# Building two one-hot groups within the head, and gate logits on VectorE, in a graph layer with a mixture of experts

## The chip, the cores and the metric

The kernel runs on one core of one Trainium2 chip. The metric is the device time of one execution in microseconds (us). A core has TensorE (PE in the profile), VectorE (DVE), ScalarE (ACT), GpSimd (POOL) and SyncE (SP, which only issues DMAs here). Each engine takes its instructions in order; they wait for one another through semaphores.

## What is computed

```python
def layernorm(x): return (x - mean(x)) / sqrt(var(x) + 1e-5)      # over the 256 features
# x [3125, 256]; src, dst [50000], sorted by dst; edge_weight [50000]
msgs = layernorm(x)[src] * edge_weight[:, None]
agg = segment_sum(msgs, dst, 3125)
x = x + agg @ W.T + b                                            # W [256, 256]
z = layernorm(x)
gates = softmax(z @ gW + gb)                                     # 4 experts
topv, topi = top_k(gates, 2); topw = softmax(topv)
shared = mlp(z; 256 -> 256 -> 128 -> 256, relu)
experts = mlp_e(z; 256 -> 128 -> 64 -> 256, relu), e = 0..3
x = x + shared + sum over the two chosen experts of topw * expert
```

All of it is float32.

## The kernel before, in words

**Tiles and units.** The 3,125 nodes are 25 tiles of 128. They are worked in 14 units of one or two tiles: G0 to G9 (the first 2,229 nodes, "gathered") and D0 to D3 ("dense"). The order of the units is `UNIT_ORDER`, "G0 D0 G1 G2 D1 G3 G4 G5 D2 G6 G7 G8 D3 G9".

**Head.** SP loads x in groups; PE multiplies x by the centred weight (L1098), ScalarE scales the product by each row's 1/std (L906) into `xn_all` and stores it as a table in DRAM (L866). VectorE takes the row statistics (`statistics(g)`, L1402, L1406), counts where each window of edges begins (`count_smaller`, with PE's `count`), and checks the edges (`edge_faults`). `choose_path` writes a flag for which all engines wait.

**Gathered units.** GpSimd gathers the source rows of 12 chunks of 128 edges (one batch; the last batch has 6): three batches of raw x (L818), then 21 from the table (L834), 246 gathers. The rows have a ring of three batches: batch b waits for `s_used`, which PE raises in batch b - 3. VectorE makes for each batch a selector (`selectors`, L1581, L1585) and a placement (L1593); PE multiplies both (`select_batch` L1155, `merge` L1191). The raw batches also need row statistics (`row_statistics`, L1532, L1536, for 12 chunks) and two transposing steps (`rawturn`, `rawlin`).

**Dense units.** For each window of five nodes SP loads a record of 128 edges (L741, 1.5 KB in 128 short pieces). VectorE splits a block of records into keys (`split_records`, L1601 to L1622). For each group of four windows VectorE makes `high_node` (`onehots`, L1635) and ScalarE `low_1h` (`low_halves`, L920, L924), PE multiplies them (`build_group`, L1209), ScalarE copies the result into `dense` (`copy_built`, L970), and PE multiplies `dense` by `xn_all` (`multiply`, L1222). Dense unit 0 has 13 groups and is multiplied tile by tile: its first 25 products need groups 0 to 6. Record blocks are of 16 windows (`BLOCKS`).

**After the sum** every unit goes through residual, statistics, `norm` (L1678), `turn` (L1234), `xt` (L989), `gated` (gate logits, L1244, on PE), layers 1 to 3 (L1264, L1273, L1277, L1311 to L1314), and on VectorE `route` (L1689 to L1694), `rank`, `mix`, `turned`, `weigh`, `finish`.

**The order of the work.** What each engine does after the flag is a list that `schedule()` (L181) works out when the kernel is built: it takes the steps' costs, start times and due times (`done`, `free`) and ranks (`RANKS`), and picks step by step. The engines run their list in order, without looking ahead. What stands ahead of the lists is written by hand: on VectorE `split_records(0)`, onehots 0 and 1, row statistics, shifts, selectors and placement of batch 0 (after `choose_path`); on ScalarE `low_halves` 0 and 1 and `row_deviation(0)` after the last table store. PE builds groups 0 and 1 as the first items of its list.

```python
            load_records(0)
            sp.dma_start(src_all[:, 0:N_CHUNKS - 1], src).then_inc(s_src, 16)
            sp.dma_start(w_all[:, 0:N_CHUNKS - 1], wgt).then_inc(s_wgt, 16)
            load_records(1)
            sp.wait_ge(s_table, 16 * len(groups))
```

Of the kernel before, what the change touches and what calls it, by code (L numbers as in the profile page):

```python
# [6 lines left out]
P = 128  # L7
# [69 lines left out]
         for v in range(4)]  # L77
WINDOWS = [-(-u.tok // WIN) for u in DENSE]
# [55 lines left out]
def users_of(b):  # L134
# [4 lines left out]
BLOCKS = [(v, t0, min(BLOCK, LOADED[v] - t0)) for v in range(len(DENSE))  # L139
          for t0 in range(0, LOADED[v], BLOCK)]  # L140
# [18 lines left out]
def block_of(v, g):  # L159
    return [(w, t0 // BLOCK) for w, t0, _ in BLOCKS].index((v, g * GROUP // BLOCK))  # L160


BANKS = 2
EARLY, FORE = 2, 4
# [5 lines left out]
RANKS = {"open": 3, "near": 0.105, "behind": 0.46, "dve_behind": 0.83, "act_behind": 1.65, "hurry": -2.49,  # L170
         "batch": 5.25, "rawturn": 14.77, "rawlin": -17.2, "merge": 7.43, "windows": 19.55, "built": 0.44,
         "rowstd": 15.95, "rawxt": -2.24, "rawout": 12.98, "low": 22.59, "select": 3.55,
         "select_late": -1.3, "place": -20.25, "records": 11.53, "onehot": -3.9, "rowstats": 5.81,
         "rowshifts": -8.25}
BUILD_RANKS = (2.58, 16.22, -1.26, -10.69)
MULT_RANKS = (-5.54, -8.91, 10.79, 17.88)
# [4 lines left out]
def schedule():  # L181
# [7 lines left out]
    done, units, left = {("load", 0): 31.0, ("load", 1): 46.0, ("load", 2): 59.5, ("load", 3): 62.5, ("records", 0): 36.0,  # L189
            ("select", 0): 46.0, ("place", 0): 46.2}, [], {}  # L190
    done.update({("begin", v): 28.5 for v in range(1, len(DENSE))})
    done.update({("onehot", k): 37.4 + 1.1 * k for k in range(EARLY)})
    done.update({("low", k): 39.3 + 1.9 * k for k in range(EARLY)})
# [3 lines left out]
    nxt = {"batch": 0, "windows": 0, "select": 1, "place": 1, "build": 0, "built": 0, "onehot": EARLY, "low": EARLY,  # L197
           "records": 1, "mult": 0, "load": FORE, "store": 0, "rowstats": 1, "rowstd": 1, "rowshifts": 1,
# [30 lines left out]
    def unit_steps(u):  # L229
        q, T, half = units.index(u), u.T, max(0.42, u.tok / PAIR)  # L230
        one = units[q - 1] if q else None
# [15 lines left out]
        else:  # L247
# [7 lines left out]
            ("dve", "norm", 0.33 * T, lambda: needs(of("std"), prior("turn", one))),  # L255
# [166 lines left out]
def build(nc, x, x_cols, src, src_tail, dst, dst_tail, nxt, nxt_tail, wgt, wgt_tail, rec, gnn_wt, packed, every, out, force_general=False):  # L422
# [5 lines left out]
    with ExitStack() as ctx:  # L428
# [249 lines left out]
        def built_in(k):  # L678

            if k % BANKS == 0:  # L680
                return build_ps
# [13 lines left out]
        def stores_before(n):  # L695
            return sum(stores_of(unit) for unit in UNITS[:n])
# [1239 lines left out]
```

## Time and profile before

| | us |
|---|---|
| median of 3 runs (lowest, highest) | 399.25 (397.38, 399.33) |
| profiled execution, whole | 398.72 |
| its span, first to last instruction | 396.6 |

```profile
PE   4998579999999999999999999999999999899984
PEld 3786457868787888888796877787878877767772
DVE  6659998984799698514688455462175442446541
ACT  2554795494388788504999532322049231244331
POOL 7777777777777777777777777777777777772000
PEclk9998668999999999999999999999999999999999
DMA  6999745944444544543343434343433344332000
```

The span is cut into 40 slices of 9.9 us; a digit is the busy share of a slice in tenths (9 is 90% or more), PEclk the granted TensorE clock in tenths of full speed. PEld is PE's loading of weights, which runs beside PE.

### The profile page before, as it was taken

The numbers are of one execution on the slowest core, as the hardware profiler recorded it, in microseconds if no ns is written. First come the engines' busy times: TensorE is split into PE (matmuls) and PEld (weight loads), VectorE is DVE, ScalarE is ACT, GpSimd is POOL, SyncE is SP. The second block draws the span as 40 slices with busy tenths as digits, with TensorE's granted clock in tenths as the row PEclk, the third lists the DMA queues.
The fourth block names the chain that finished last, engine by engine and source line by source line (L and its number), as shares of the span: only waits on it lengthen the run. The fifth ranks groups of instructions, "written<-read, shape, count | busy, mean of one in ns | idle before, by whom it ended". The sixth has DMA issues, their size and how long they took to land.

```text
span 396.6 us, 8051 instructions
## 1 busy us (share of the span) xinstructions
PE 367.7 (93%) x2419; PEld 295.9 (75%) x2419; DVE 243.5 (61%) x1013; ACT 202.0 (51%) x551; POOL 273.5 (69%) x294
## 2 busy tenths in 40 slices
PE   4998579999999999999999999999999999899984
PEld 3786457868787888888796877787878877767772
DVE  6659998984799698514688455462175442446541
ACT  2554795494388788504999532322049231244331
POOL 7777777777777777777777777777777777772000
PEclk9998668999999999999999999999999999999999
DMA  6999745944444544543343434343433344332000
GB/s 183 379 380 279 210 111 131 341 106 105 105 108 118 129 118 100 133 106 108 104 130 102 132 107 134 105 129 105 132 103 107 115 125 134 105 108 80 15 13 25
DMA packets 53855, 53.15 MB, mean 134 GB/s; under 512 B 32522, under 2 KB 43636, under 8 KB 53684
## 3 DMA queue, kind: packets, MB, share of 16 engines
q0 software_dynamic: 13536, 36.98, 31.8%
q1 hardware_dynamic: 35220, 10.01, 10.9%
q10 hardware_dynamic: 5056, 5.64, 4.1%
q8 instruction: 21, 0.34, 0.4%
q14 instruction: 22, 0.18, 0.1%
HBM read 46.12 MB, written 6.48 MB: 133 GB/s over the span
## 4 chain that ended last, share of the span: by engine, by line
PE 82%; ACT 6%; DMA 5%; DVE 3%; issue 2%; SPq 1%; ACTq 0%; DVEq 0%
PE agg_ps L1222 19%; PE hid_ps L1264 17%; PE window_ps L1155 8%; PE tok_ps L1313 5%; DMA x_sb<-in_x 5%; PE build_ps L1209 5%; PE agg_ps L1191 5%; PE agg_ps L1209 4%; PE tok_ps L1311 3%; PE hid_ps L1277 3%; PE hid_ps L1273 3%; PE mid_ps L1244 3%; ACT low_1h L920 2%; PE hid_ps L1209 2%; PE mid_ps L1234 1%
## 5 line engine op out<-in xcount | busy, mean ns | idle before, releaser
L834 POOL DMA_INDIRECT rows<-normalised_rows,src_all x246 | 236.2, 960 | 75.5 <-issue 74.3
L1222 PE MATMUL agg_ps<-xn_all,dense 128*128 128x256 f32 x350 | 80.3, 381 | 0.8 <-ACT dense L970 0.8
L1222 PEld LDWEIGHTS agg_ps<-xn_all,dense 128*128 128x128 f32 x350 | 65.3, 190 | 11.0 <-ACT dense L970 1.7
L1264 PE MATMUL hid_ps<-xt,pack 128*128 128x256 f32 (+2 forms) x336 | 71.4, 358 | 0.0
L1264 PEld LDWEIGHTS hid_ps<-xt,pack 128*128 128x128 f32 x336 | 56.4, 190 | 9.1 <-issue 3.6
L920 ACT ACTIVATE low_1h<-iota,lo_f 128x128 f32<-128x128 f32 x182 | 57.6, 393 | 0.5 <-ACT xn_all L906 0.5
L1635 DVE TENSOR_SCALAR high_node<-iota,hi_f,own_w 128x125 f32<-128x125 f32 x182 | 49.4, 357 | 4.5 <-PE build_ps L1209 2.9
L1008 ACT ACTIVATE h<-hid_ps,pack 128x256 f32<-128x256 f32 (+2 forms) x84 | 32.8, 441 | 37.4 <-PE hid_ps L1264 37.2
L818 POOL DMA_INDIRECT rows<-in_x,src_first x36 | 34.9, 968 | 11.0 <-issue 10.4
L1155 PE MATMUL window_ps<-rows,select 128*32 128x256 f32 x564 | 37.3, 394 | 0.9 <-DVE select L1585 0.9
L1209 PE MATMUL build_ps<-high_node,low_1h 128*128 128x125 f32 x184 | 27.8, 299 | 4.6 <-ACT low_1h L924 3.6
L1209 PEld LDWEIGHTS build_ps<-high_node,low_1h 128*128 128x128 f32 x184 | 25.5, 212 | 7.9 <-issue 5.6
L924 ACT ACTIVATE low_1h<-low_1h 128x512 f32<-128x512 f32 (+1 forms) x46 | 28.8, 626 | 1.5
L1155 PEld LDWEIGHTS window_ps<-rows,select 128*32 128x32 f32 x564 | 16.5, 112 | 15.3 <-issue 5.2
L1799 DVE TENSOR_TENSOR y<-tok_ps,x 128x512 f32<-128x512 f32 (+1 forms) x14 | 8.9, 633 | 28.6 <-PE tok_ps L1314 28.6
L1313 PE MATMUL tok_ps<-pack,h 128*128 128x256 f32 (+1 forms) x100 | 25.7, 378 | 0.0
L970 ACT ACTIVATE dense<-build_ps 128x500 f32<-128x500 f32 x23 | 14.6, 636 | 20.7 <-PE agg_ps L1222 18.6
L1581 DVE TENSOR_TENSOR select<-slots,rel 128x384 f32<-128x384 f32 (+1 forms) x24 | 13.2, 550 | 15.8 <-PE window_ps L1155 15.7
L951 ACT ACTIVATE windows<-window_ps 128x256 f32<-128x256 f32 (+1 forms) x24 | 9.1, 378 | 25.8 <-PE window_ps L1155 25.8
L1191 PE MATMUL agg_ps<-windows,place 128*128 128x256 f32 (+1 forms) x92 | 21.8, 382 | 0.0
L1313 PEld LDWEIGHTS tok_ps<-pack,h 128*128 128x128 f32 (+1 forms) x100 | 18.7, 187 | 3.0
L1191 PEld LDWEIGHTS agg_ps<-windows,place 128*128 128x128 f32 (+1 forms) x92 | 16.9, 190 | 2.3 <-issue 0.3
(172 smaller groups left out, 523.2 us busy)
## 6 DMA issues: line engine op xcount, KB each, us to landing
rows<-normalised_rows,src_all POOLq DMA_INDIRECT x246, 2.8
x_sb<-in_x SPq DMA_DIRECT2D x6, 512.0 KB, 9.0
normalised_rows<-xn_all ACTq DMA_DIRECT2D x6, 512.0 KB
records<-in_rec SPq DMA_DIRECT2D x184, 1.5 KB
out<-y SPq DMA_DIRECT2D x10, 256.0 KB
dense<-in_x_cols ACTq DMA_DIRECT2D x4, 512.0 KB, 9.9
pack<-in_packed SPq DMA_DIRECT2D x1, 1544.5 KB, 9.9
x_sb<-in_x SPq DMA_DIRECT2D x3, 256.0 KB
```

What stands on the lines that cost most here:

```text
L818: pool.indirect_dma_start(rows[:, b * BATCH + pos, :], None, x[:, :], bass.IndirectOffsetOnAxis(ap=src_first[:, c:c + 1], axis=0)).then_in ...
L834: pool.indirect_dma_start(rows[:, b % RING * BATCH + pos, :], None, table[:, :], bass.IndirectOffsetOnAxis(ap=src_all[:, c:c + 1], axis=0) ...
L920: last = act.activation(low_1h[:, k % RING, j, :], iota[:, 0:P], ACT.Abs, scale=-1.0, bias=lo_f[:, at + j:at + j + 1])
L924: act.activation(low_1h[:, k % RING, 0:n, :], low_1h[:, k % RING, 0:n, :], ACT.Relu, scale=-1.0, bias=1.0).then_inc(s_low, 1)
L1008: last = act.activation(u.h1[:, m, 0:tok], by_half(u.hid_ps[k % 2])[:, m % 2, 0:tok], ACT.Relu, bias=b1_sb[:, m:m + 1])
L1155: last = pe.matmul(window_ps[SLOT * g:SLOT * (g + 1), 0:D], select[:, b % RING, j, :], rows[:, b % RING * BATCH + pos, :], start=(i == 0), ...
L1191: last = pe.matmul(sums_of(unit)[:, t * D:(t + 1) * D], place[0:full, b % KEEP, at:at + P], windows[0:full, b % KEEP, :], start=(b == batc ...
L1209: last = pe.matmul(built_in(k)[:, j * width:(j + 1) * width], low_1h[:, k % RING, j, :], high_node[:, k % RING, j, :], start=True, stop=True)
L1222: last = pe.matmul(dense_ps[0:r, t * D:(t + 1) * D], dense[:, h, t * P:t * P + r], xn_all[:, h, :], start=(h == 0 and t == 0), stop=(h == ...
L1264: last = pe.matmul(by_half(u.hid_ps[b % 2])[:, m % 2, 0:tok], w, u.xt[:, k, 0:tok], start=(k == 0), stop=(k == KD - 1))
L1313: pe.matmul(o, u.h2[:, 1 + k, c], ew3_sb[:, k, :], start=False, stop=False)
L1635: last = dve.tensor_scalar(high_node[:, r, j, :], iota[:, 0:HI * WIN], hi_f[:, at + j:at + j + 1], own_w[:, at + j:at + j + 1], ALU.is_equ ...
```

## The change

It does four things:

1. Record blocks: the first block of 16 windows becomes two of 8 (`HEAD_BLOCK`), so there are 15 blocks. SP issues the same loads in the same order (blocks 0 and 1 ahead of src and w, block 2 behind them, block 3 after the table).
2. On VectorE `split_records(0)` and `onehots(0)` now stand between `statistics(5)` and `statistics(6)`, `onehots(1)` behind `statistics(6)`; after `choose_path` come `split_records(1)`, `row_statistics(0)`, `onehots(2)`, `row_shifts(0)`, `selectors(0)`, `placement(0)`. On ScalarE `low_halves(0)` stands ahead of the last deviation, `low_halves(1)` ahead of the scaling of product 11; after the flag come two `copy_built`, `low_halves(2)` and `row_deviation(0)`. PE builds group 0 behind the product of pair 10 and ahead of `count(3)`, group 1 behind the last product. Three groups are one-hot ahead of the lists instead of two.
3. The gate logits of all units but D3, G8 and G9 (`LAST_UNITS`) are made on VectorE, four `tensor_tensor_reduce` of 256 elements a tile, with the bias as start value; `gated` on PE and the bias add in `route` go away for these eleven units (21 tiles). The transposed gate weights come with the broadcast load `shared`, which grows from 130 KB to 642 KB.
4. The lists are made anew, with other ranks and start times. They begin so (unit or number behind each step):

```
PE before:  build 0, 1, batch 0, build 2, 3, rawturn 0, rawlin 0, build 4, 5, 6, batch 1, mult 0 (25 of them),
            build 7, 8, 9, batch 2, build 10, batch 3, rawturn 1, build 11, rawlin 1, build 12, merge G0, batch 4, mult 0 (25)
PE after:   build 2, batch 0, build 3, rawturn 0, rawlin 0, build 4, 5, batch 1, build 6, 7, rawturn 1, mult 0 (2), rawlin 1,
            mult 0 (23), batch 2, build 8, batch 3, build 9, 10, 11, batch 4, merge G0, build 12, rawturn 2, ...
DVE before: onehot 2, 3, records 1, rowstats 1, onehot 4, 5, rowshifts 1, onehot 6, 7, select 1, place 1, rowstats 2, ...
DVE after:  onehot 3, rowstats 1, records 2, rowshifts 1, onehot 4, 5, 6, select 1, place 1, onehot 7, rowstats 2,
            records 3, rowshifts 2, onehot 8, bias G0, onehot 9, 10, select 2, place 2, ...
ACT after:  low 3, built 2, windows 0, built 3, rawxt 0, rowstd 1, rawout 0, low 4, 5, 6, built 4, 5, low 7, windows 1,
            rowstd 2, built 6, 7, rawxt 1, ...
```

In the list after, the steps of G0 stand among the second 25 products of unit 0 (before: behind them), and all steps of G2 up to `spr` ahead of the products of unit 1 (before: up to `l1b`). From batch 22 on both lists of PE are the same.

```diff
+LAST_UNITS = [DENSE[-1], *GATHERED[-2:]]
+HEAD_BLOCK = 2 * GROUP
+BLOCKS = [(0, t0, HEAD_BLOCK) for t0 in range(0, BLOCK, HEAD_BLOCK)]
+BLOCKS += [(v, t0, min(BLOCK, LOADED[v] - t0)) for v in range(len(DENSE))
+           for t0 in range(0 if v else BLOCK, LOADED[v], BLOCK)]
-EARLY, FORE = 2, 4
+EARLY, FORE = 3, 5
-    free = {"pe": 36.6, "act": 44.9, "dve": 46.2, "sp": 65.0}
+    free = {"pe": 39.2, "act": 44.1, "dve": 46.1, "sp": 65.0}
...
+    done.update({("onehot", k): (30.0, 32.5, 44.8)[k] for k in range(EARLY)})
+    done.update({("low", k): (31.4, 37.6, 42.5)[k] for k in range(EARLY)})
...
-            ("pe", "gated", 0.24 * T, lambda: needs(of("xt"))),
+        ] + ([
+            ("pe", "gated", 0.41 * T, lambda: needs(of("xt"))),
+        ] if late else []) + [
...
+            ("dve", "gates", 1.63 * T, lambda: needs(of("norm"))),
...
-        row_stats = sb("row_stats", [P, ROW_SLOTS, 6])
+        row_stats = dst_i[:, 0:6 * ROW_SLOTS].bitcast(F32).rearrange("p (j s) -> p j s", s=6)
...
+            if GROUPS[k][0] < TILE_BY_TILE:
+                return u.hid_ps[k % BANKS]
+            return dense_ps if k % BANKS else build_ps
...
-                sp.dma_start(shared[:, :], every.to_broadcast([P, D + E])).then_inc(s_linear, 16)
+                sp.dma_start(shared[:, :], every.to_broadcast([P, D + E * D + E])).then_inc(s_linear, 16)
...
             load_records(0)
+            load_records(1)
             sp.dma_start(src_all[:, 0:N_CHUNKS - 1], src).then_inc(s_src, 16)
             sp.dma_start(w_all[:, 0:N_CHUNKS - 1], wgt).then_inc(s_wgt, 16)
-            load_records(1)
+            load_records(2)
             sp.wait_ge(s_table, 16 * len(groups))
...
+                if p == 9:
+                    low_halves(0)
                 if p in DEVIATIONS:
                     deviations(DEVIATIONS.index(p))
+                if p == len(pairs) - 1:
+                    low_halves(1)
...
-            for k in range(EARLY):
-                low_halves(k)
-            row_deviation(0)
+            act.wait_ge(s_flag, 1)
+            for k in range(BANKS):
+                copy_built(k)
+            low_halves(BANKS)
+            row_deviation(0)
...
                 multiply_x(p)
+                if p == 10:
+                    build_group(0)
                 if p == 1:
                     count(0)
...
+            build_group(1)
             pe.wait_ge(s_flag, 1)
...
+            def gates(q):
+                done = E * gated_tiles(q)
+                dve.wait_ge(s["xn"], q + 1)
+                for t in range(UNITS[q].T):
+                    for e in range(E):
+                        if done >= 2:
+                            dve.wait_ge(s_gate_x, done - 1)
+                        dve.tensor_tensor_reduce(
+                            out=gate_x[:, done % 2, :], in0=u.xn[:, t, :], in1=gate_w_sb[:, e, :], scale=1.0,
+                            scalar=gate_b_sb[:, e:e + 1], op0=ALU.mult, op1=ALU.add,
+                            accum_out=u.logit[:, t, e:e + 1]).then_inc(s_gate_x, 1)
+                        done += 1
...
             statistics(5)
             split_records(0)
-            for k in range(EARLY):
-                onehots(k)
+            onehots(0)
+            statistics(6)
+            onehots(1)
+            edge_places()
+            count_smaller(3)
+            edge_faults()
+            for v in range(1, len(DENSE)):
+                begin_windows(v)
+            choose_path()
+            split_records(1)
             row_statistics(0)
+            onehots(2)
             row_shifts(0)
             selectors(0)
             placement(0)
```

## Rows read from the trace of the kernel before

**Rows 1.** the page, parts 1 and 5: busy time; the gathers (busy, mean ns).

```profile
PE 367.7 (93%) x2419; PEld 295.9 (75%) x2419; DVE 243.5 (61%) x1013; ACT 202.0 (51%) x551; POOL 273.5 (69%) x294
...
L834 POOL DMA_INDIRECT rows<-normalised_rows,src_all x246 | 236.2, 960 | 75.5 <-issue 74.3
```

**Rows 2.** timeline of PE (start us, us): one unit's gate products; batch 23.

```profile
315.07 0.95 PE L1244 MATMUL mid_ps<-pack,xt 128*128 128x4 f32 x8
315.88 1.97 PE L1264 MATMUL hid_ps<-xt,pack 128*128 128x256 f32 x8
...
369.48 1.49 PE L1155 MATMUL window_ps<-rows,select 128*32 128x256 f32 x12
```

**Rows 3.** the same 246 gathers by line: ns min/median/max; landing.

```profile
L834 POOL DMA_INDIRECT rows<-normalised_rows,src_all x246: 941/946/1287, 49.4 to 359.7; - x123
...
DMA to landing us min/median/max: 2.7/2.8/3.8
```

**Rows 4.** timeline of POOL: three of its gathers.

```profile
49.36 0.95 POOL L834 DMA_INDIRECT rows<-normalised_rows,src_all  x1 [0.36 <-PE window_ps L1155]
...
82.95 1.23 POOL L834 DMA_INDIRECT rows<-normalised_rows,src_all  x1 [0.30 <-issue]
...
359.75 0.95 POOL L834 DMA_INDIRECT rows<-normalised_rows,src_all  x1 [0.30 <-issue]
```

**Rows 5.** timeline of DVE in the head, with what ended its idle time.

```profile
29.54 1.41 DVE L1402 BATCH_NORM_STATS2 stats<-x_sb 128x6 f32<-128x256 f32 x4 [3.00 <-DMA x_sb<-in_x]
...
31.28 0.42 DVE L1480 SCALAR_TENSOR_TENSOR rel<-dst_f,tok_ps 128x282 f32<-128x282 f32 x1
...
37.71 0.15 DVE L1601 TENSOR_SCALAR hi_i<-records 128x16 int32<-128x16 int32 x1
...
38.89 2.14 DVE L1635 TENSOR_SCALAR high_node<-iota,hi_f,own_w 128x125 f32<-128x125 f32 x8
40.95 4.00 DVE L1532 BATCH_NORM_STATS2 row_stats<-rows 128x6 f32<-128x256 f32 x12
...
46.51 0.17 DVE L1544 TENSOR_TENSOR row_w<-w_all,row_rstd 128x12 f32<-128x12 f32 x1 [0.62 <-ACT row_rstd L875]
...
47.84 0.34 DVE L1593 TENSOR_SCALAR place<-iota,posn 128x256 f32<-128x256 f32 x1
```

**Rows 6.** SP's record loads; DMA queue 1 in 27:31 and in 31:36 us.

```profile
17.05 9.24 SPq L741 DMA_DIRECT2D records<-in_rec  x8
...
q1 hardware_dynamic: 907, 0.04, 14.5%
...
q1 hardware_dynamic: 1150, 0.01, 13.5%
```

**Rows 7.** timeline of ACT in the head.

```profile
39.72 1.02 ACT L906 ACTIVATE xn_all<-build_ps,zero,rstd 128x256 f32<-128x256 f32 x2 [1.64 <-PE build_ps L1098]
...
41.21 1.28 ACT L920 ACTIVATE low_1h<-iota,lo_f 128x128 f32<-128x128 f32 x4 [0.47 <-ACT xn_all L906]
42.52 0.63 ACT L924 ACTIVATE low_1h<-low_1h 128x512 f32<-128x512 f32 x1
```

**Rows 8.** timeline of PE, head and first product of dense unit 0.

```profile
43.25 2.04 PE L1209 MATMUL build_ps<-high_node,low_1h 128*128 128x125 f32 x8 [3.56 <-ACT low_1h L924]
...
47.98 2.79 PE L1155 MATMUL window_ps<-rows,select 128*32 128x256 f32 x24 [0.86 <-DVE select L1585]
...
65.42 11.06 PE L1222 MATMUL agg_ps<-xn_all,dense 128*128 128x256 f32 x50 [0.77 <-ACT dense L970]
```

**Rows 9.** windows: length; busy of PE, PEld, DVE, ACT, POOL; clock; DMA share, GB/s.

```profile
89.70:160.60 70.90, 70.33 (x500) 58.93 (x498) 55.41 (x252) 50.20 (x143) 53.84 (x57) 1.00 0.48 113
```

**Rows 10.** timeline of DVE: two SBUF sources, one source, and a bias add.

```profile
33.81 0.56 DVE L1495 SCALAR_TENSOR_TENSOR dense<-dst_f,y 128x391 f32<-128x391 f32 x1
...
35.15 0.55 DVE L1509 TENSOR_REDUCE faults<-dense 128x1 f32<-128x391 f32 x1
...
82.69 1.27 DVE L1648 TENSOR_TENSOR x_sb<-x_sb,shared 128x512 f32<-128x512 f32 x2
```

More of the change, by code:

```diff
@@ L159, in block_of @@
 def block_of(v, g):
-    return [(w, t0 // BLOCK) for w, t0, _ in BLOCKS].index((v, g * GROUP // BLOCK))
+    return [w == v and t0 <= g * GROUP < t0 + n for w, t0, n in BLOCKS].index(True)
 BANKS = 2
-EARLY, FORE = 2, 4
+EARLY, FORE = 3, 5
 STATS_BEHIND = 3
 UNIT_ORDER = "G0 D0 G1 G2 D1 G3 G4 G5 D2 G6 G7 G8 D3 G9"
[L170 to L176, printed above, removed]
+RANKS = {"open": 3, "near": 0.14, "behind": 0.22, "dve_behind": 0.45, "act_behind": 2.16, "hurry": -5.23,
+         "batch": 1.25, "rawturn": 8.65, "rawlin": -25.18, "merge": 5.81, "windows": 2.09, "built": 0.6,
+         "rowstd": -2.64, "rawxt": 2.76, "rawout": 9.65, "low": 17.47, "select": 1.64, "select_late": 7.66,
+         "place": -23.18, "records": 8.69, "onehot": 0.56, "rowstats": 25.05, "rowshifts": -11.68}
+BUILD_RANKS = (4.99, 16.77, -0.42, -10.85)
+MULT_RANKS = (0.36, -9.88, 8.93, 15.94)
 GATHER_US = 1.256
@@ L196, in schedule @@
     waiting = [named[name] for name in UNIT_ORDER.split()]
-    nxt = {"batch": 0, "windows": 0, "select": 1, "place": 1, "build": 0, "built": 0, "onehot": EARLY, "low": EARLY,
-           "records": 1, "mult": 0, "load": FORE, "store": 0, "rowstats": 1, "rowstd": 1, "rowshifts": 1,
+    nxt = {"batch": 0, "windows": 0, "select": 1, "place": 1, "build": BANKS, "built": BANKS, "onehot": EARLY, "low": EARLY,
+           "records": 2, "mult": 0, "load": FORE, "store": 0, "rowstats": 1, "rowstd": 1, "rowshifts": 1,
            "rawturn": 0, "rawxt": 0, "rawlin": 0, "rawout": 0}
@@ L652, in build @@
         s_off = sem("s_off")
+        s_gate_x = sem("s_gate_x")
         s_keys = sem("s_keys")
@@ L696, in stores_before, with gates_before, tops_before, gated_tiles @@
             return sum(stores_of(unit) for unit in UNITS[:n])
+        def gates_before(n):
+            return sum(unit not in LAST_UNITS for unit in UNITS[:n])
+        def tops_before(n):
+            return 2 * n - gates_before(n)
+        def gated_tiles(n):
+            return sum(unit.T for unit in UNITS[:n] if unit not in LAST_UNITS)
         def gathered_before(n):
@@ L1115, in edge_bases, with build_group @@
                 last.then_inc(s_base, 1)
+            def build_group(k):
+                v, g = GROUPS[k]
+                pe.wait_ge(s_onehot, k + 1)
+                pe.wait_ge(s_low, k + 1)
+                if k >= BANKS:
+                    pe.wait_ge(s_build_copied, k - BANKS + 1)
+                if v and k % BANKS:
+                    pe.wait_ge(s["x1"], last_before(DENSE[v], "D"))
+                width = HI * WIN
+                for j in range(min(GROUP, WINDOWS[v] - g * GROUP)):
+                    last = pe.matmul(built_in(k)[:, j * width:(j + 1) * width], low_1h[:, k % RING, j, :],
+                                     high_node[:, k % RING, j, :],
+                                     start=True, stop=True)
+                last.then_inc(s_built, 1)
             pe.wait_ge(s_pad, 2)
@@ L1881, in _ @@
                     normalise(q)
+                    if UNITS[q] not in LAST_UNITS:
+                        gates(q)
                     route(q)
```

121 lines of the change are left out of this document (51 added, 70 removed).

## The prediction

> **What bounds the kernel now.** I read the page first. TensorE is busy 367.7 of 396.6 us, VectorE 243.5 and GpSimd 273.5 [rows 1]. After the first product of dense unit 0 at 65.4 us [rows 8] the timeline of PE has no gap over 0.9 us, so each microsecond of PE work taken out there is one off the end, unless something else ends last. So the second reading is of what PE could run into. GpSimd issues its 246 table gathers as one chain, one each 1.25 us: first 49.36, last 359.75 [rows 4]. A gather lands 2.8 us after its issue [rows 3]: 362.5, or 363.5 if that counts from the end of its 0.95 us. PE starts batch 23, which needs it, at 369.48 [rows 2]. The slack is 6.0 to 6.9 us, and behind batch 23 both lists are the same, 27.1 us long. So a gain above some 6.5 us can't be had, and every microsecond by which the gather chain starts later or runs slower comes off that slack. The chain's start is not GpSimd's own: the first table gather reuses the rows of batch 0 and waited for PE's batch 0 [rows 4], PE started that at 47.98 on the selectors of VectorE [rows 8].
>
> **The sum's base.** The profiled execution took 398.72 us with a span of 396.6, so 2.1 us lie around it. It is 0.5 us under the median of the three runs (399.25). A measurement of this kernel can tell about 0.5%, 2.0 us.
>
> **Gate products.** Eight records of a two-tile unit run from 315.07 to 315.88 [rows 2]: 0.81 us, 0.101 each. Eleven units with 21 tiles lose them: 84 records, 8.5 us of PE, all on PE's path. The wait for xt before them stays, since l1a needs xt too. Term on PE: -8.5.
>
> **First groups in the head.** SP's order of DMAs is unchanged, only the blocks are 8, 8 and 16 windows, so the moved steps hang on when the first eight record loads land. SP issues them from 17.05 to 26.3, and DMA queue 1 then moves 907 packets in 27 to 31 us and 1,150 in 31 to 36 with almost no bytes [rows 6], which is records (128 short packets a load). 1,150 packets are the last eight loads; so the first eight are through at about 31.1. The same queue holds the x tiles, the last of which ended a 3.0 us wait at 29.54 [rows 5]. The list of the change puts the wait for records ahead of statistics(6), on an engine that runs in order. [...]
>
> VectorE, from 31.1: split 1.18 (37.71 to 38.89) and four one-hots 1.05 (half of the eight, 38.89 to 40.95) to 33.35; statistics(6) 1.74 (29.54 to 31.28) to 35.1; four one-hots to 36.15. The places, fault and begin steps through the flag, 6.43 (31.28 to 37.71), end at 42.6, against 37.7. Then the new second split 1.18, row statistics 4.86 (40.95 to 45.81), onehots(2) 1.05, weights, selectors and placement 1.67 (46.51 to 48.18) [rows 5]: 51.35 against 48.18. Of these 3.2 us, 1.05 are work done ahead, 1.18 the extra split, the rest wait.
> ScalarE: low_halves(0) is ahead of the last deviation and holds it only to 33.8; statistics(6) ends at 35.1, so that costs 2 to 4 us. PE's count(3) stands behind VectorE's fourth count, 4.9 later, so the last product's scaling goes from 39.72 to about 44.6 [rows 7] and the last table store from 40.8 to 45.6. Who waits: SP for the table before block 3, weights and shifted tiles (some 3 us later, used after 90 us, hidden); GpSimd not, it is free at 49. Two copies 1.1, low_halves(2) 1.94 (41.21 to 43.15, [rows 7]) and the row deviation end at 50.0; the selectors need that: 51.4 again. PE has build 2 ahead of batch 0 and starts it at 51.4 to 51.9. I take 3.5 us later than 47.98. So the gather chain starts 3.5 us later. Nothing in its path gives that back.
>
> PE up to its first dense product: placement 51.6, onehot 3 1.05, row statistics(1) 4.86, split 1.18, three groups of one-hots 3.15, selectors and place 1.5, onehot 7 1.05, row statistics(2) 4.9, ScalarE's deviation 0.5 and copy of group 6 0.5 give 70.4, against 65.4 [rows 8]: +5.0. Ahead of it PE has now done build 7 and rawturn 1, 1.1 us by the times of such steps later on (a build is half of [rows 8]'s 2.04 at full clock). Two builds of 2.04 that used to stand at 43 to 47 are covered by the VectorE wait; that they lie in the head gains nothing while the selectors set the end of it. Term on PE: +4.0; if records landed by 28 it would be about +1.
>
> **Gates on VectorE.** 84 tensor_tensor_reduce of 256 elements. No such operation is in the trace. Below: a statistics instruction of 256, 4.00/12 = 0.33 [rows 5]; above: a scalar_tensor_tensor with two SBUF sources and 391 elements, 0.56 [rows 10]. I take 0.37, that row scaled by 256/391: 31 us, less eleven small logit adds. Over the whole that leaves VectorE under 70%. In the stage from the first table batches to the first product of dense unit 1, 89.7 to 160.6, it is busy 55.4 of 70.9 [rows 9]; there it gets the gates of G0, D0, G1 and G2 (7 tiles, 10.4 us) and the rank and mix of G2, which used to lie beside the products of unit 1 (about 3.1): 69, while PE's own work there shrinks to 68. With no room left each in-order wait on VectorE (records, a residual) reaches PE through one-hots, selectors or mix. Its cost is between 0 (lists shift work well) and 8 us (half of the 15.5 us that VectorE idled there stays idle). I take 3, nearer to the low end because PE has products to run beside. Term on PE: +3.0.
> [...] A scalar_tensor_tensor of 391 elements with two f32 sources took 0.56 here and a one-source reduction of 391 0.55 [rows 10], so no halving shows in that one; with the accumulator it is not in the trace.
>
> **At nothing.** The shared load grows by 512 KB and, with SP held by the table, lands some microseconds later; VectorE has the bias of G0 behind onehot 8 and ahead of the selectors of batch 2, but PE runs 11.06 us of products meanwhile [rows 8]. Without that cover the wait would hold batch 2 and with it the gathers. Groups 0 and 1 use banks that the transposes of x have left long before. The reuse of dst_i for row statistics, the merged semaphores and the wait of norm for the gates (same engine, in order) cost nothing: the gates stand ahead of that norm anyway.
>
> **Contention.** A gather that started at 82.95 took 1.23 instead of 0.946, while the two-source bias adds ran from 82.69 [rows 4, 10]. All 246 lie above the median by 246 x (960 - 946) ns = 3.4 us [rows 1, 3], and two-source VectorE work beside them is about 33 us (selectors and bias adds). 31 us more of it, in shorter pieces, would add at most 3.2 and at least 0; I take 1.5. [...]
>
> **Sum.** PE alone: -8.5 + 4.0 + 3.0 = -1.5. Gather chain: 3.5 + 1.5 = 5.0 against a slack of 6.0 to 6.9: -1.0 to -1.9. Both come to about -1.5: a span of 395.1, with 2.1 around it 397.2.
>
> **Rivals.** (a) The records are there when VectorE asks (about 28), and the 3.0 us wait hides the split and first group. Then placement is at 48.6, the gather chain loses 0.5 + 1.5 and ends -4.5; PE: -8.5 + 1 + 3 = -4.5. 394.2. For it: the planner's constants say the split is done at 28.5 and VectorE free at 46.1; against it: the packets of [rows 6].
> (b) Slower: VectorE becomes the bound from 89.7 to 160.6. The end moves later once its waits there cost PE over 4.5 us, measurably over 6.5; at 8, PE alone has -8.5 + 4 + 8 = +3.5: 402.2. For it: 69 us of work for 68 of time; against it: the list was made anew around these costs.
> (c) A gate instruction takes twice my price: 0.37 more in each of the 28 of that stage, 10.4 us, PE alone +8.9: 407.6. [Rows 10] speak against it.
> (d) The two ends cancel: new waits eat exactly the products saved, 398.7.
>
> **How the numbers follow.** Forecast 0.37, (a) 0.26, (b) 0.20, (c) 0.04, (d) 0.13. Faster by over 0.5% is below 396.7: (a) and a third of the forecast's case, 0.38. Slower is above 400.7: (b), (c) and a little of (d) and the forecast, 0.28. Same 0.34. The range from 392.8 to 402.2 takes in (a) with its PE term smaller, and (b); the forecast's own is 395.5 to 399.5.
>
> **What would show it.** In the new profile: VectorE waiting for records ahead of statistics(6), the flag near 42.6, placement near 51, the first table gather near 52.9 and the last near 364.7, PE's first dense product near 70, gate instructions of 0.33 to 0.42, PE waits for VectorE or ScalarE between 90 and 165, and PE close to the gathers at batch 23. Wrong if the split starts before 29, if the last gather is issued before 362, or if PE waits for rows by several microseconds at the end.

## The result, and the profile after

The changed kernel took 402.72 us (median of 4 runs, 401.92 to 403.88) against 398.31 for the kernel before in the same measurement: a ratio of 1.0112, 95% interval 1.007 to 1.0155. It is slower by about 1.1%, outside the range of the prediction (392.8 to 402.2). The profiled execution took 402.8 us with a span of 400.7, 4.1 more than before.

The page of the changed kernel, the rows that answer to [rows 1], with the row of the gate instructions (busy us, mean ns):

```profile
PE 360.9 (90%) x2335; PEld 286.6 (72%) x2335; DVE 273.9 (68%) x1179; ACT 201.2 (50%) x551; POOL 277.0 (69%) x294
...
L860 POOL DMA_INDIRECT rows<-normalised_rows,src_all x246 | 239.9, 975 | 82.1 <-issue 74.4
L1700 DVE CUSTOM_DVE_ANT_0 gate_x<-xn,shared 128x256 f32<-128x256 f32 x84 | 35.0, 479 | 0.1
```

PE has 84 instructions and 6.8 us of busy time less, and ends later. So the products are gone and something else has taken the end. The chain of waits says what:

```profile
POOL 52%; issue 18%; PE 11%; DVE 9%; SPq 5%; DMA 3%; ACT 1%; POOLq 0%; DVEq 0%
```

In the kernel before the same view was

```profile
PE 82%; ACT 6%; DMA 5%; DVE 3%; issue 2%; SPq 1%; ACTq 0%; DVEq 0%
```

Now the chain that ended last runs along GpSimd's gathers. In the view of the gathers by line, PE never waited for one before; in the changed kernel it waited 2.2 us in five places. Their timeline (start us, us), to be read beside [rows 4]:

```profile
47.90 0.95 POOL L844 DMA_INDIRECT rows<-in_x,src_first  x1 [0.30 <-issue]
54.73 0.94 POOL L860 DMA_INDIRECT rows<-normalised_rows,src_all  x1 [5.88 <-PE window_ps L1204]
...
86.71 0.95 POOL L860 DMA_INDIRECT rows<-normalised_rows,src_all  x1 [1.81 <-PE window_ps L1204]
...
369.86 0.95 POOL L860 DMA_INDIRECT rows<-normalised_rows,src_all  x1 [0.30 <-issue]
```

and PE's batch 23 ([rows 2]):

```profile
372.76 1.49 PE L1204 MATMUL window_ps<-rows,select 128*32 128x256 f32 x12
```

The last gather is issued 10.1 us later than before. That is three things: 5.37 at the first gather (54.73 for 49.36), 1.05 more idle time where the gathers wait for PE's batch 2 (1.81 at 86.71, for 0.76 at 80.20 before), and 3.7 by which the gathers themselves are longer (the sum of what each takes over 0.946 us is 7.2 for 3.5). Before, batch 23 stood 9.7 us behind the last issue; now it stands 2.9 behind it, which is the landing time of a gather counted from its issue [rows 3]. 10.1 of delay met 6.9 of slack, batch 23 is 3.3 us later, and the tail behind it is 27.9 us for 27.1: 4.1. The row of before at batch 2:

```profile
80.20 0.94 POOL L834 DMA_INDIRECT rows<-normalised_rows,src_all  x1 [0.76 <-PE window_ps L1155]
```

Where the first 5.4 us come from is in VectorE's head, beside [rows 5]:

```profile
32.31 0.17 DVE L1608 TENSOR_SCALAR hi_i<-records 128x8 int32<-128x8 int32 x1 [6.60 <-DMA records<-in_rec]
...
33.43 1.11 DVE L1642 TENSOR_SCALAR high_node<-iota,hi_f,own_w 128x125 f32<-128x125 f32 x4
34.47 1.39 DVE L1433 BATCH_NORM_STATS2 stats<-x_sb 128x6 f32<-128x256 f32 x4
...
44.17 0.28 DVE L1554 TENSOR_REDUCE worst<-mid_ps 1x1 f32<-1x128 f32 x1 [0.98 <-PE mid_ps L1188]
...
52.91 0.35 DVE L1600 TENSOR_SCALAR place<-iota,posn 128x256 f32<-128x256 f32 x1
```

VectorE stands 6.6 us in front of records that have not landed, with the last statistics behind them; placement ends at 53.3 (48.18 before). ScalarE's last scaling, behind those statistics, is at 46.63 ([rows 7]: 39.72). PE's batch 0 starts at 53.34 and its first dense product at 72.23 ([rows 8]: 47.98 and 65.42).

The windows view of the stage that answers to [rows 9], the same stretch of the work some 5 to 8 us later (length; busy of PE, PEld, DVE, ACT, POOL; clock; DMA share, GB/s):

```profile
95.00:168.70 73.70, 72.29 (x500) 58.84 (x499) 65.13 (x296) 51.36 (x147) 56.02 (x59) 1.00 0.49 115
```

VectorE is 88% busy there, up from 78%, and PE has 1.4 us idle in 73.7 (0.6 in 70.9 before): VectorE is close to full and hardly holds PE.

PE's new waits for other engines lie 120 us further on. From 284 to 315 us of before and from 288 to 318 us of the changed kernel (the last dense unit's groups are built there), with the longest waits of PE in the second stretch:

```profile
284.00:315.00 31.00, 30.27 (x211) 24.78 (x210) 15.53 (x57) 16.57 (x44) 23.38 (x26) 1.00 0.37 107
288.00:318.00 30.00, 25.35 (x178) 19.56 (x177) 22.42 (x93) 16.39 (x45) 22.97 (x24) 1.00 0.36 106
```

```profile
296.25 1.13 PE L1158 MATMUL agg_ps<-high_node,low_1h 128*128 128x125 f32 x8 [0.93 <-DVE x L1668]
...
304.86 1.16 PE L1158 MATMUL agg_ps<-high_node,low_1h 128*128 128x125 f32 x8 [1.03 <-DVE high_node L1642]
...
315.83 0.39 PE L1331 MATMUL tok_ps<-mix_t,owner 79*128 79x256 bf16 x2 [0.78 <-DVE mix_t L1808]
```

PE is idle 4.65 us of the 30 there (0.52 of it for rows), and 0.7 of the 31 before.

### The profile page after: what moved, and what is told of

It reads as the page before. It is cut to its first block, busy times and chain, and to the rows that moved or that the text cites. A ratio compares the mean times of both kernels' runs of the same rounds, so it can differ in the third digit from the quotient of the medians.

```text
span 400.7 us, 8062 instructions
## 1 busy us (share of the span) xinstructions
PE 360.9 (90%) x2335; PEld 286.6 (72%) x2335; DVE 273.9 (68%) x1179; ACT 201.2 (50%) x551; POOL 277.0 (69%) x294
## 4 chain that ended last, share of the span: by engine, by line
POOL 52%; issue 18%; PE 11%; DVE 9%; SPq 5%; DMA 3%; ACT 1%; POOLq 0%; DVEq 0%
POOL rows L860 52%; PE agg_ps L1254 3%; DVE dst_i L1563 3%; DMA records<-in_rec 2%; DVE high_node L1642 2%; PE hid_ps L1294 2%; SPq L754 1%; SPq L744 1%; SPq L766 1%; PE window_ps L1204 1%; PE agg_ps L1129 1%; PE tok_ps L1343 1%; DMA rows<-normalised_rows,src_all 1%; DVE row_mv L1567 1%; PE tok_ps L1341 1%
## 5 line engine op out<-in xcount | busy, mean ns | idle before, releaser
L860 POOL DMA_INDIRECT rows<-normalised_rows,src_all x246 | 239.9, 975 | 82.1 <-issue 74.4
L1254 PE MATMUL agg_ps<-xn_all,dense 128*128 128x256 f32 x350 | 83.2, 385 | 3.1 <-ACT dense L996 3.1
L1700 DVE CUSTOM_DVE_ANT_0 gate_x<-xn,shared 128x256 f32<-128x256 f32 x84 | 35.0, 479 | 0.1
L1158 PE MATMUL hid_ps<-high_node,low_1h 128*128 128x125 f32 x104 | 17.0, 318 | 10.3 <-DVE high_node L1642 7.4
L1158 PEld LDWEIGHTS hid_ps<-high_node,low_1h 128*128 128x128 f32 x104 | 15.0, 221 | 13.7 <-DVE high_node L1642 11.3
L1668 DVE TENSOR_TENSOR x<-agg_ps,x_sb 128x512 f32<-128x512 f32 (+1 forms) x14 | 8.8, 630 | 20.4 <-PE agg_ps L1254 16.4
L1158 PE MATMUL agg_ps<-high_node,low_1h 128*128 128x125 f32 x132 | 18.2, 280 | 3.0 <-DVE high_node L1642 1.8
## 6 DMA issues: line engine op xcount, KB each, us to landing
dense<-in_x_cols ACTq DMA_DIRECT2D x4, 512.0 KB, 10.1
```

Of the source, the lines that this page charges most:

```text
L860: pool.indirect_dma_start(rows[:, b % RING * BATCH + pos, :], None, table[:, :], bass.IndirectOffsetOnAxis(ap=src_all[:, c:c + 1], axis=0) ...
L1158: last = pe.matmul(built_in(k)[:, j * width:(j + 1) * width], low_1h[:, k % RING, j, :], high_node[:, k % RING, j, :], start=True, stop=True)
L1254: last = pe.matmul(dense_ps[0:r, t * D:(t + 1) * D], dense[:, h, t * P:t * P + r], xn_all[:, h, :], start=(h == 0 and t == 0), stop=(h == ...
L1700: dve.tensor_tensor_reduce(out=gate_x[:, done % 2, :], in0=u.xn[:, t, :], in1=gate_w_sb[:, e, :], scale=1.0, scalar=gate_b_sb[:, e:e + 1], ...
```

## The experiments

Theory A: the chain of gathers sets the end; the head makes it start late, and the gate instructions lengthen it a little. Theory B: VectorE, nearly full from 95 to 170 us, holds PE. All ratios are to the kernel before on the same chip; four kernels were measured together each time, runs 1 to 4, 5 to 8 and 9 to 12, on three chips.

**1. Four gathers less in the changed kernel.** The cut takes four gathers out of the chain in its early part (batch 7, quad 1), and touches nothing else. The output lacks those edges.

```diff
-                        for pos, j in quad(b, i):
+                        for pos, j in [] if (b, i) in SKIP else quad(b, i):    # SKIP = {(7, 1)}
```

> The changed kernel with four of the 246 table gathers left out (those of the second third of batch 7; their rows keep what was there, so some nodes get wrong sums). Theory A, GpSimd's gather chain sets the end: four gathers of 1.25 us are 5.0 us less of it; the last gather is issued near 364.9 instead of 369.9, batch 23 starts near 367.8 instead of 372.8, and the whole takes 397.7 to 398.5 instead of 402.7, the lower end if PE alone has that much room. Theory B, VectorE and PE between 95 and 170 us set the end: the chain is shorter but the time stays within 1 us of 402.7.

Measured: 399.07 us, ratio 1.004 (1.0013 to 1.0068), where the changed kernel with all gathers has 1.0105 to 1.0112. That is 0.6 us above the times that were expected, so PE alone had less room than theory A gave it. Its gathers and PE at the end:

```profile
365.47 0.95 POOL L861 DMA_INDIRECT rows<-normalised_rows,src_all  x1 [0.30 <-issue]
```

```profile
370.39 1.49 PE L1205 MATMUL window_ps<-rows,select 128*32 128x256 f32 x12
```

Batch 23 is now 4.9 us behind the last issue: PE comes later than the rows. So PE alone ends where it is seen here, and the difference to the changed kernel, 0.65 to 0.7%, is what the gathers hold back (the two were measured on different chips).

**2. The same cut in the kernel before.**

> The kernel before with the same four gathers left out. Both theories: no change (within 0.8 us), since the chain there had 6.9 us of slack against batch 23; the last gather near 354.7. If it gets faster by several us, the slack was not there and the reading of landings is wrong.

Measured: 396.43 us, ratio 0.9987 (0.9952 to 1.0023): nothing. There the last gather is issued at 357.00 and batch 23 starts at 366.73. The cut is free where the gathers have slack. How much there was is another matter: the last issue was expected at 354.7, and the gathers' sum over 0.946 us is 6.2 in this profile, not 3.5. With the four gathers (5.0 us) put back, batch 23 would stand 4.7 behind the last issue, which is by that estimate 1.8 us of slack and not 6.9.

**3. Gates with one source.** The 84 multiply-and-sum instructions become plain sums over one source, so that the logits leave out the gate weights.

```diff
-                        dve.tensor_tensor_reduce(
-                            out=gate_x[:, done % 2, :], in0=u.xn[:, t, :], in1=gate_w_sb[:, e, :], scale=1.0,
...
+                        dve.tensor_reduce(u.logit[:, t, e:e + 1], u.xn[:, t, :], AX_X,
+                                          ALU.add).then_inc(s_gate_x, 1)
```

> The changed kernel with each of the 84 gate instructions replaced by a one-source sum of the same 256 elements (the gate weights and bias are left out, so the gates are wrong); VectorE's work should stay about the same length, 0.41 a step. Theory A with contention: the gathers' excess over 0.946 us falls from 7.2 to about 3.5 us in sum, the last gather comes near 366.2 and the whole takes 3.0 to 3.7 us less, 399.0 to 399.7. If contention is not from the second SBUF source: excess stays near 7 and the time at 402.7. Theory B: no change in time beyond 1 us whatever the gathers do.

Measured: 400.96 us, ratio 1.0096 (1.0057 to 1.0136). In the median it can't be told from the changed kernel: the 3.0 to 3.7 us less that theory A expected did not come. The timelines are finer: every gather that takes over 0.97 us began while a VectorE instruction was running. In the changed kernel 8 such gathers began inside a gate instruction and are 1.5 us over in sum; over the nine profiles with these gates it is 6 to 9 gathers with 1.0 to 1.75 us. In this kernel none did. The first of them in the changed kernel with the next gather, on POOL, and the gates on DVE:

```profile
99.33 1.15 POOL L860 DMA_INDIRECT rows<-normalised_rows,src_all  x1 [0.31 <-issue]
100.79 0.95 POOL L860 DMA_INDIRECT rows<-normalised_rows,src_all  x1 [0.30 <-issue]
```

```profile
99.19 0.48 DVE L1700 CUSTOM_DVE_ANT_0 gate_x<-xn,shared 128x256 f32<-128x256 f32 x1
99.59 0.08 DVE L1700 DVE_READ_ACCUMULATOR2_ANT logit<- 128x1 f32 x1
99.59 0.48 DVE L1700 CUSTOM_DVE_ANT_0 gate_x<-xn,shared 128x256 f32<-128x256 f32 x1
...
100.40 0.48 DVE L1700 CUSTOM_DVE_ANT_0 gate_x<-xn,shared 128x256 f32<-128x256 f32 x1
```

The gather at 99.33 began 0.14 us into a gate instruction and is 0.2 us over, though three more gate instructions start beside it; the one at 100.79 began 0.39 into one and is not over at all. In the changed kernel the starts at 0.14, 0.20 and 0.26 us are 0.21, 0.15 and 0.10 over, and no start under 0.06 or from 0.38 on is over. In each of the eight, start and excess add up to 0.35 to 0.36 us, and over the nine profiles, with 72 such gathers, to 0.34 to 0.36. In this run 16 gathers began 0.10 to 0.28 us into a one-source sum, and none is over by more than 0.01 us. So of the 3.7 us by which the chain grew, gates are about 1.5. The total of this kernel is still 6.3, where 3.5 was expected, mostly at selectors, bias adds and one-hots (2.3, 1.4 and 1.1 us). The rest of the 3.7 is not the change's for certain: run 8 gives 4.9 for the kernel before where its first profile gave 3.5.

**4. The head of before, gates on VectorE.** Blocks of 16 records, the first two groups made after `choose_path` and built in PE's list; all behind that as in the changed kernel.

```diff
             statistics(5)
-            split_records(0)
-            onehots(0)
             statistics(6)
-            onehots(1)
             edge_places()
...
             choose_path()
-            split_records(1)
+            split_records(0)
+            onehots(0)
+            onehots(1)
             row_statistics(0)
-            onehots(2)
```

> The head of the kernel before (blocks of 16 records, groups 0 and 1 split and made behind the flag, PE builds them first in its list), with the changed kernel's list and gates on VectorE otherwise. Theory A: the first table gather is back at 49.4 to 50, batch 2 no longer holds the chain by more than 0.5, the last gather comes near 363.5 (359.75 plus 3.7 of contention), and the whole near 396 to 397 unless PE alone ends later. Theory B: the stage from 95 to 170 us has the same work, so most of the 4 us stays: 401 or more.

Measured: 399.47 us, ratio 1.005 (1.0022 to 1.0079). A bit over half of the 1.1% comes back, and the kernel is still slower than before: neither the 396 to 397 of theory A nor the 401 of theory B. Its profile (397.08, the lowest of its ten runs) has the first table gather at 50.10 with 0.74 idle before it, the last at 364.46 and batch 23 at 368.13: within a microsecond of the landing. And PE's batch 0 is at 48.71 although placement was done at 44.7:

```profile
46.74 2.04 PE L1161 MATMUL hid_ps<-high_node,low_1h 128*128 128x125 f32 x8 [4.54 <-ACT low_1h L958]
48.71 2.79 PE L1204 MATMUL window_ps<-rows,select 128*32 128x256 f32 x24
...
223.42 1.94 PE L1204 MATMUL window_ps<-rows,select 128*32 128x256 f32 x16 [4.28 <-DMA rows<-normalised_rows,src_all]
```

The last row shows that the gathers held PE before batch 23 already. The new list has build 2 ahead of batch 0, and build 2 waits for ScalarE. That gave a new question, taken up in runs 7 and 11.

**5. Old head and four gathers less.**

> The head of before, the rest of after, and four of the 246 table gathers left out (quad 1 of batch 7; those edges' sums are missing from the output). Theory A (the chain of gathers sets the end of the changed kernel, its head by starting the chain late, the 84 gate instructions by lengthening it): with the old head PE alone should come to batch 23 some 7 us before it does in the kernel before (84 products less, 1 to 1.5 us lost to VectorE), and four gathers less bring the last issue from 364.5 to about 359.5, so batch 23 near 362.5 and an end 4 to 6 us before that of the old head with all gathers: 1 to 1.5% faster than the kernel before. Theory B (the stage in which VectorE is overfull sets the end): under 1 us from the skipped gathers, 0 to 0.5% slower than before, as the old head with all gathers was.

Measured: 392.94 us, ratio 0.9886 (0.9846 to 0.9927). Last issue 358.36, batch 23 at 363.29, again 4.9 behind it. This is the change without its head and nearly without the limit of the gathers: gates on VectorE with their list could be worth 1.1%. Theory B expected 1.000 to 1.005 here and falls. Run 2 had shown that the cut itself is worth nothing where PE sets the end.

**6. The new head alone, gates on PE.** `LAST_UNITS` holds all units, and the list is planned anew with the ranks of after (which were not found for this kernel, so its list need not be its best).

```diff
-LAST_UNITS = [DENSE[-1], *GATHERED[-2:]]
+LAST_UNITS = [*DENSE, *GATHERED]
```

> The head of after, but all gate products on TensorE again, and the list planned anew for that with after's ranks. Theory A: the chain of gathers starts as late as in after (54.7 to 57.3), its excess is that of before and not 1.5 us more, so gathers end about 1.5 us earlier than in after; but PE has its 8.5 us back on top of a first dense product at about 72 to 73, so PE alone sets batch 23, at about 377, and the time is 1.5 to 2% above before (some 403). Theory B (gates on VectorE are what costs): back to before, within 0.5%.

Measured: 405.29 us, ratio 1.0201 (1.0136 to 1.0266), as theory A has it. The sum was right, its place was not: batch 23 came at 371.30, 5.3 behind the last issue, not at 377, since this list puts more work behind it (32.3 us of tail, where run 8 has 26.7), and the records landed early in this profile (30.59). With this list the new head costs 2%, and gates on VectorE give back half of that. Of the 9.8 us by which this span is longer than that of run 8, 5.6 lie in the tail, so the head alone costs less than 2%; how much less no run measured. The kernel also waits once for the weights ahead of the first gate products, which costs nothing in this profile: the load is issued at 66.76 and lands 9.6 us later, and those products start at 98.74 with no idle time before them.

**7. The gather chain first.** As run 4, but row statistics, selectors and placement of batch 0 ahead of the first one-hots, `row_deviation(0)` ahead of the low halves, batch 0 ahead of the builds.

```diff
             choose_path()
-            split_records(0)
-            onehots(0)
-            onehots(1)
             row_statistics(0)
+            split_records(0)
             row_shifts(0)
             selectors(0)
             placement(0)
+            onehots(0)
+            onehots(1)
```

> The head of before with its own order changed: row statistics, selectors and placement of batch 0 stand ahead of the first one-hots on VectorE, the row deviation ahead of the low halves on ScalarE, and batch 0 ahead of the first builds on PE; rest as after (gates on VectorE). Theory A: placement(0) ends 2 to 3 us earlier than in before, the first table gather is issued near 47 instead of 50.1, the last near 361.5, batch 23 comes 2.5 to 3 us earlier than with the old head, and the time is about 0.7% less than that kernel's: 0.2 to 0.6% faster than before, if PE's first dense product stays near 66. Theory B: no gain from an earlier chain, 0.5% slower than before as the old head was.

Measured: 396.2 us, ratio 0.9962 (0.9933 to 0.999). The gain is as expected and the way is not: batch 0 starts at 42.33, but the first table gather stays at 49.78, because GpSimd is still issuing its raw gathers one each 1.25 us until then. An earlier batch 0 buys slack in front of that point, no earlier start. The 2 to 3 us by which the expectation moved the chain were not there.

**8. The kernel before, unchanged.**

> The kernel before, unchanged, for its profile on the same chip. Theory A: the sum by which its table gathers exceed 0.946 us, read on this chip, is 1.5 us or more below that of the kernels with gates on VectorE (7.2 to 7.9), and batch 23 comes 7 us or more after the last gather's issue. If the sum is already near 6, the difference of 3.7 us between the first two profiles was half the chip's.

Measured: 395.87 us once. Batch 0 starts on PE at 45.52 (47.98 in the profile of before), yet the first table gather is at 49.76, and the last at 361.11; batch 23 at 367.09, 6.0 behind it. The kernel before has its gather chain full from the raw gathers on. Where batch 0 holds the first table gather, that starts 1.39 us behind it (changed kernel, run 4); by that batch 0 had no room in the first profile and some 2.8 us in this one. The gathers' sum over 0.946 is 4.9. So the slack at batch 23 is 3.1 us here. Theory A had expected 7 us or more behind the last issue; the kernel before is nearer to its gathers than its first profile says. That profile also has the latest head of three: the flag at 37.8 (34.9 in run 2, 35.4 here), PE's first dense product at 65.42 (62.67, 63.03). PE's path from there to batch 23 is the same in all three, 304.06 us.

**9. The changed kernel again, with the next three.**

> The changed kernel, unchanged, on the chip of the next three. Theory A and B alike: 0.7 to 1.5% above before. VectorE's split of the first records starts where the loads land, 30.6 to 34.4 in the profiles so far, and the first table gather is issued 22.4 to 22.9 us behind that start.

Measured: 401.28 us, ratio 1.0105 (1.0072 to 1.0137). Split at 32.32, first table gather 54.87, last 369.39, batch 23 at 372.24: 2.85 behind.

**10. The last statistics ahead of the split.**

```diff
             statistics(5)
+            statistics(6)
             split_records(0)
             onehots(0)
-            statistics(6)
             onehots(1)
```

> The changed kernel with statistics(6) ahead of the first split of records and both first one-hot groups behind it, so that the 1.74 us of statistics lie inside the wait for records. Theory A: the first table gather is issued about 20.8 us behind the start of the split instead of 22.6, ScalarE's last scaling comes 2 to 3 us earlier, and the time is 1.5 to 2.5 us (0.4 to 0.6%) below that of after on this chip, since gathers and PE's first dense product both follow. Theory B: the head is not in the path, no change to after.

Measured: 399.85 us, ratio 1.0077 (1.0041 to 1.0113); beside run 9 1.4 us or 0.3% less, in the direction of theory A and just under its size (1.5 to 2.5). The intervals overlap, so the gain rests on the profiles: first table gather 52.68, 20.7 behind the split at 31.96 (22.6 in run 9), last 366.72, batch 23 at 369.60, 2.6 earlier than in run 9. The first gather is 2.2 earlier (0.4 of it because the records landed earlier), the wait for batch 2 is gone (1.56 at 86.90 in run 9), and the gathers are 0.8 longer. Work put into the wait comes off the end.

**11. Batch 0 ahead of build 2.** As run 4, one item moved in PE's list.

```diff
-ORDER["pe"] = [("build", 0), ("build", 1)] + ORDER["pe"]
+ORDER["pe"] = [("build", 0), ("build", 1), ("batch", 0)] + [i for i in ORDER["pe"] if i != ("batch", 0)]
```

> The old head with gates on VectorE, as in the first old-head run, but batch 0 ahead of build 2 in PE's list, as it stood in the kernel before. In the old-head run build 2 waited for ScalarE's low halves until 46.7 and batch 0 came at 48.7, 3.9 us behind its placement, so the gather chain had no slack against it. Theory A (that is why the old head measured 0.5% above before and the chain-first head 0.4% below): batch 0 at 45 to 46, the first table gather at 49.8 with an idle time of 0.30 before it, time equal to the chain-first kernel within 0.2%, 0.2 to 0.6% below before. Rival: contention of the gates alone explains the old head's 0.5%, and this kernel stays at 0.3 to 0.6% above before.

Measured: 396.0 us, ratio 0.9956 (0.9915 to 0.9997), where run 4 had 1.005. PE, POOL, and PE at the end:

```profile
44.49 2.79 PE L1204 MATMUL window_ps<-rows,select 128*32 128x256 f32 x24 [2.06 <-DVE select L1592]
```

```profile
49.63 0.95 POOL L868 DMA_INDIRECT rows<-normalised_rows,src_all  x1 [0.30 <-issue]
...
362.24 0.95 POOL L868 DMA_INDIRECT rows<-normalised_rows,src_all  x1 [0.30 <-issue]
```

```profile
365.13 1.49 PE L1204 MATMUL window_ps<-rows,select 128*32 128x256 f32 x12
```

Moving one build from in front of batch 0 is worth 0.9% by the two ratios, which are from two chips. That the move does it is shown, its size is not explained by the profiles. Both have the flag at 34.2; batch 0 stands at 48.71 and at 44.49, and the first table gather, 50.10 and 49.63, is only 0.47 earlier. The last issue is 2.2 earlier, and 1.7 of that are shorter gathers (sum over 0.946: 7.9 and 6.2), a difference no larger than between profiles of the kernel before. The profile of run 4 is its fastest of ten; what its slower executions wait for is open. Contention of the gates (1.6 us) is in this kernel too and does not make it slower than before, so the rival falls.

**12. The chain-first kernel again.**

> The chain-first kernel once more, on the same chip as the three others. Theory A: 0.2 to 0.6% below before again, equal to the kernel with batch 0 first; 1.2 to 1.7% below after.

Measured: 396.41 us, ratio 0.9974 (0.994 to 1.0008), batch 23 2.89 behind the last issue. Runs 7, 11 and 12 are 0.3 to 0.4% faster than the kernel before (the last with an interval that reaches 1.0008), and by the ratios 1.3 to 1.5% faster than the changed one. They are the fastest of the kernels that leave nothing out, and all three end at the gathers. They keep the larger load of `shared`, the reused buffers and the gates on VectorE, so none of these makes the changed kernel slower than the one before. Run 5 shows what lies behind that limit.

## Why the prediction was wrong

The mechanism that the prediction reads as bounding was the one that decided; its terms were too small. The step that failed is the gather chain's sum, "5.0 against a slack of 6.0 to 6.9". It measured 10.1 against 6.9 in the first pair of profiles: 5.37 instead of 3.5 at the start, 1.05 instead of nothing at batch 2, and 3.7 instead of 1.5 for longer gathers.

- **The base.** Right for its profile: slack 6.9, landing 2.8 to 2.9 counted from the start of the issue, the upper of the two readings. But the slack is not a fixed property of that kernel: 3.1 in run 8, and 1.8 in run 2 with its four gathers put back. The sum stood on the profile with the most. Half wrong in its cause. The prediction says that the chain's start is not GpSimd's own, since the gather of [rows 4] waited for PE. The row has 0.36 idle where every gather has 0.30 (run 8, run 7): both ended together. With batch 0 earlier the first table gather stays where it is (run 7); with batch 0 later it moves (run 4, and the changed kernel).
- **Records and VectorE's head.** "The first eight are through at about 31.1": 32.31 in the profile, 30.6 to 34.4 over the six profiles with this head, and in each of the six the first table gather came 20.7 to 22.9 us behind it. The packets of [rows 6] were also read a little early: 1,150 are nine loads of 128, not eight, so the first eight end after 31. From split to flag I summed 11.5 us, it took 12.2 (a wait of 0.98 for PE's transposed faults was not in it); from there to the end of placement 8.75, it took 8.7. Placement 51.35 became 53.3.
- **The chain's start.** "I take 3.5 us later" became 5.37. 1.9 of it is the line above.
- **"At nothing": batch 2.** The prediction let 11 us of dense products cover it. PE's head was 6.8 us late, not 5.0, batch 2 on PE came at 85.77 (79.26 before), and GpSimd waited 1.05 more. A cover was named, but it stands in PE's order behind the delayed head and moved with it.
- **Contention.** "I take 1.5": the gates' own part is 1.5 in that profile by the gathers that began inside one (1.0 to 1.75 over nine profiles), right. The chain grew by 3.7 in all. The other 2 us lie at other VectorE instructions, and profiles of the kernel before differ by as much (3.5, 4.9 in run 8, 6.2 with the cut of run 2). The prediction had set gate work beside all gathers' excess in proportion; in the nine profiles all 72 gathers that are over at a gate instruction had begun 0.10 to 0.27 us into it, 6 to 9 in each profile, and the sum follows their number. A slack of 1 to 2 us was thinner than this spread, and the sum took no account of that. 
  Run 3 bears on the second source: with one source no gather was held at a gate instruction (16 began 0.10 to 0.28 us into one, none over by more than 0.01 us). That one source always spares a gather is not shown: the one-hots have one tensor source too, and in the changed kernel 12 gathers that began inside one are 0.9 us over in sum.
- **Gates' price.** 0.37 was taken; 0.41 us from one to the next, 0.48 for one with its 0.08 read of the accumulator beside it. Within the bounds (0.33 to 0.56). 
  The doubled price of rival (c) does not show: 0.48 us for 256 elements with an accumulator stands to 0.56 for 391 without one [rows 10], where a doubled price would be 0.74.
- **The overfull stage.** "I take 3". PE goes from its first dense product to batch 23 in 304.06 us before and in 296.75 and 297.51 in runs 1 and 5, where gathers don't hold it: 6.6 to 7.3 less. With 8.5 of products and 1.1 of builds done ahead, the lists cost PE 2.3 to 3.0 over that way. The number is right, and by luck: in the stage that the prediction names PE has 1.4 us of idle time for 0.6 before, 0.8 more. The rest comes from 288 to 318 us, 4.1 us of waits for VectorE and ScalarE for 0.7 before (4.1 in each of the nine profiles with these gates), less some 1.6 that PE idles less behind that.
- **PE's own term.** -8.5 + 4.0 + 3.0 = -1.5 was predicted. The start was 6.8 late, 5.7 with the 1.1 taken off, so the sum is -8.5 + 5.7 + 2.3 to 3.0, about 0. Even without gathers the change gains nothing. Against the two other profiles of the kernel before, whose first dense product is at 62.67 and 63.03, the start is 9.2 to 9.6 us late and PE alone loses 2 to 3 us by the same sum. Run 1's 1.004 says the same.
- **Rivals.** (a) needed records at 28, and they never came before 30.6. (c) falls with the 0.41 us of a gate. (b) is 402.2, near the 402.72 measured, and its mechanism was not what happened: VectorE had 8.6 us of idle time in that stage and PE had 1.4. A forecast that goes wrong in the direction of my own mechanism, by 3 to 5 us, was not among the rivals; it should have been the one on the slower side, with its point at 6.9 us of added delay.

## What to carry to other kernels

Where one engine works at 93% and a second, with an in-order chain of issues, comes a few us ahead of it at the end (6.9 in one profile here, 3.1 and 1.8 by two others), the chain is the next bound: take that distance from more than one profile, write down what the change adds to the chain's start and to its length, and compare that with the spread of those terms between runs, not with their middle. Work that is moved ahead in an engine's order takes its wait with it (6.6 us for the records on VectorE in the changed kernel, 4.5 for the low halves on PE in run 4); put it behind everything that does not need it (statistics first, batch 0 before build 2), above all in a head on whose end another engine's whole chain hangs. And test a suspected chain by making it shorter: four gathers out of 246 told within one measurement what the gathers cost in each kernel.

## What the runs showed that was not expected

- A gather that takes 0.946 us alone took 1.15 when it began 0.15 us into a two-source VectorE instruction of 0.48 us, also when more such instructions followed directly. One that began 0.26 us in was 0.10 over, one that began 0.38 us in was not over. Start and excess add up to 0.34 to 0.36 us in all 72 such gathers of the nine profiles, not to the 0.48 of the instruction.
- The first eight small record loads were issued by 21.5 to 24.9 us and had landed at 30.6 to 34.4, in six profiles of the same head. Landing did not follow issue: 21.61 went with 30.59, 21.49 with 32.32.
- PE's way from its first dense product to batch 23 took 304.06 us in each of three profiles of the kernel before; what varied were the head and the gathers.
- Runs 4 and 11 differ by the place of one item in one list, and their ratios by 0.9%.
